# Banded attention: the third and fourth head's scores ahead of three projections, the last group's scores around the norm's transposes, adds ahead of lookups

## Chip, cores and metric

The kernel runs on one core of a Trainium2 chip. The metric is the device time of one execution in microseconds (us), as the median of three runs. The engines are called as the profile calls them: PE is TensorE (matrix products), DVE is VectorE, ACT is ScalarE, POOL is GpSimd, SP is the engine that only issues transfers here.

## The reference, cut to what matters

The program is a two-layer decoder; only the first of its six stages is touched: windowed attention with rotary positions, added to the residual stream. Per batch element (4 of them) there are 512 tokens of width 512, 16 query heads of width 128 in 4 groups, and one key/value head for each group.

```python
x = x + _L0_attn_ref(_layernorm(x, axis=-1), wq, wk, wv, wo)
...
q = jnp.einsum('bth,oh->bto', x, wq).reshape(B, T, Q_HEADS, HEAD_DIM)   # 16 heads
k = jnp.einsum('bth,oh->bto', x, wk).reshape(B, T, KV_HEADS, HEAD_DIM)  # 4 heads
v = jnp.einsum('bth,oh->bto', x, wv).reshape(B, T, KV_HEADS, HEAD_DIM)
q = _apply_rope(q, cos, sin)
k = _apply_rope(k, cos, sin)
scores = jnp.einsum('btgrd,bsgd->bgrts', qg, k) * scale
allowed = (idx[None, :] <= idx[:, None]) & (idx[:, None] - idx[None, :] <= WINDOW)   # WINDOW = 128
scores = jnp.where(allowed[None, None, None], scores, jnp.finfo(scores.dtype).min)
probs = jax.nn.softmax(scores, axis=-1)
out = jnp.einsum('bgrts,bsgd->btgrd', probs, v)
return jnp.einsum('bto,ho->bth', out, wo)
```

A later stage needs feed-forward weights that are given as 4-bit indices into a table of 16 values (`lut[gate_idx]` and so on). The kernel looks these up on DVE during the attention stage and stores them to memory for the later stage.

## The kernel before, in words

The attention stage is `stage_window_attention`. It makes one pass per batch element (three in a hardware loop, `more` true, and the last one outside of it, `more` false), and each pass goes over the 4 groups `g`. Each engine has its own program (`one_pass`, once for each engine); the engines meet through semaphores. No scheduler moves anything: the order on an engine is the order in which the code is written, and every engine runs its instructions strictly in that order.

The work of one group:

- Scores. PE computes the masked scores of the group's 4 heads (`scores`, lines 508 and 511) into two slots of PSUM. Heads 1 and 3 use one slot, heads 2 and 4 the other, so PE may begin head 3 only when ACT has taken the exponentials of head 1 out of the slot, and head 4 after those of head 2. DVE takes the row maxima (`maxima`, line 680), turns them into a bias (line 682), ACT takes the exponentials and row sums (`exponentials`, line 602), DVE the reciprocal of the sums (`inverse`, line 687), and POOL multiplies the probabilities by it (`probabilities`, line 759, four instructions for a head).
- Projections for the next group. Between the scores PE projects the next group's key k and its four queries q1 to q4 (`project`, line 491, `nxt` in the code). Each result goes through rotary encoding on three engines: ACT copies it with its halves exchanged (`swap`, lines 615 and 616), DVE multiplies the projection by the cosine (`rope`, line 675), POOL multiplies the exchanged copy by the sine (line 750) and adds both (line 753).
- Weighing. When the probabilities of all 4 heads are ready (PE waits for `prob_ready`), PE transposes them (`turn_probs`, line 521), multiplies by v (`weigh`, line 531), and by the output weights (line 574). DVE adds the four 128-row tiles to the residual x (line 729): these are "the adds".
- Four lookups on DVE in each group (`lookup.pick`, lines 364, 367 and 373, and `lookup.choose`, line 383). `pick` makes 4 masks and 8 choices between table values, `choose` reduces 8 candidates to 1 with 7 predicated copies; SP then stores the result and fetches new indices. A lookup is done by `pick` and `choose` of the same number, and one lookup must end before the next begins. Both inputs of a predicated copy, the mask and the values, are in SBUF.

In the third group of a pass DVE normalizes x for the next pass (`norm_stats`, `norm_apply`, with a power on POOL between them), and in the last group PE transposes it (`norm_tensor`, line 268) before the key and the queries of the next pass can be projected from it; ACT and DVE each copy two of the four transposed blocks (`features`). After the last group PE computes v for the next pass (`values`, line 541).

All PE results but the scores go through four PSUM banks in turn (`Ring`, by a list of steps). A step may write its bank only when the engine that read the step before it on that bank has released it. The four norm transposes follow the four output tiles on the ring, so the transposes of block k wait for add k.

The stage ends with a barrier of all engines, SP among them, and SP gets there only when the last lookup's store has landed (`sync_end`). The next stage issues its loads after that barrier.

## Time and profile before

| what | value |
|---|---|
| median of three runs | 2406.33 us (2403.66 to 2410.31) |
| the profiled execution's own time | 2406.55 us |
| its span, first to last instruction | 2404.8 us |
| attention stage from the first scores to the last add | 60.95 to 927.58 us of the span |
| PE, DVE, ACT, POOL busy over the whole span | 89%, 71%, 39%, 44% |
| mean granted clock of PE | 0.962 |

The profile is of one execution. Start times are us from the span's start. A row of the timeline gives start, length, engine, line, operation, what it writes and reads, how many such instructions in a row are merged into it, and in brackets how long the engine was idle just before and whose result ended that. A matmul in 32-bit is recorded as two parts, so four matmuls of 512 columns read "x8". PE's two clock levels are 2.4 GHz (1.0 in the column PEclk) and 1.2 GHz (0.5).

### The profile page before, as it was taken

Reading aid. Unit: us, or ns where it says so; the run is one execution under the profiler, and the core shown is the slowest. Engines: PE = TensorE matmul, PEld = TensorE weight load, DVE = VectorE, ACT = ScalarE, POOL = GpSimd, SP = SyncE. Lnnn points to the kernel's source line nnn. Section 1 sums busy time; section 2 is a strip of 40 time slices with the busy share of each in tenths; the row PEclk is TensorE's granted clock in tenths of the full one; section 3 lists DMA queues with packets and bytes.
Section 4 is the critical chain, followed back from the end, with each engine's and each line's share of the span. In section 5 each row is a group of like instructions: output and inputs, shape, how many; then the busy total and the mean of one; then the engine's idle time right before and its main releaser. Section 6 shows DMA issues by size and latency. Waiting matters only on the chain. (4 is left out here: it accounts for less than half of the span.)

```text
span 2404.8 us, 24923 instructions
## 1 busy us (share of the span) xinstructions
PE 2151.0 (89%) x7344; PEld 1108.7 (46%) x7344; DVE 1712.6 (71%) x2983; ACT 944.7 (39%) x1808; POOL 1048.7 (44%) x798
## 2 busy tenths in 40 slices
PE   6998999899999977997889898999789999999858
PEld 2554445454455543443555555465333433334234
DVE  1787788768876885786889889889546364654554
ACT  1443344333333433764655646465123232332311
POOL 2343354333333440322899998999511011010142
PEclk9999999999999998998999999999889999999979
DMA  7000000000000002455644526353332122221121
GB/s 263 19 19 18 19 20 20 18 18 22 22 18 19 23 23 90 159 186 214 266 162 166 197 105 210 127 203 108 107 80 78 41 77 57 70 70 46 52 109 53
DMA packets 95563, 214.87 MB, mean 89 GB/s; under 512 B 15832, under 2 KB 33112, under 8 KB 93032
## 3 DMA queue, kind: packets, MB, share of 16 engines
q1 hardware_dynamic: 77192, 156.18, 19.8%
q10 hardware_dynamic: 17760, 57.42, 6.7%
q8 instruction: 40, 0.66, 0.1%
q14 instruction: 59, 0.48, 0.1%
q0 software_dynamic: 512, 0.13, 0.0%
HBM read 146.30 MB, written 42.07 MB: 78 GB/s over the span
## 5 line engine op out<-in xcount | busy, mean ns | idle before, releaser
L759 POOL TENSOR_SCALAR a_prob<-a_prob,a_rsum 128x256 f32<-128x256 f32 x256 | 146.6, 590 | 467.3 <-DVE a_rsum L687 467.1
L1455 POOL TENSOR_TENSOR s_state<-s_b_rows,s_delta_u 128x1024 f32<-128x1024 f32 x128 | 303.5, 2384 | 36.9 <-DMA s_b_rows<-scan_bc 34.4
L1499 DVE TENSOR_TENSOR_SCAN s_state<-s_decay,s_state 128x512 f32<-128x512 f32 x256 | 304.9, 1211 | 15.5 <-ACT s_decay L1441 13.2
L1614 PE MATMUL c_bank<-c_xn_parts,c_w_parts 128*128 128x512 f32 (+1 forms) x1056 | 269.5, 405 | 6.2 <-DMA c_w_parts<-ffn_weights_lo 6.2
L1441 ACT ACTIVATE s_decay<-s_delta,s_a 128x512 f32<-128x512 f32 x256 | 173.5, 689 | 226.1 <-DVE s_state L1499 220.6
L491 PE MATMUL a_bank<-a_xn_t,a_wq 128*128 128x512 f32 x512 | 227.3, 592 | 0.0
L602 ACT ACTIVATE a_prob<-a_score,a_neg_m 128x256 f32<-128x256 f32 x256 | 117.6, 475 | 279.0 <-DVE a_neg_m L682 278.8
L1614 PEld LDWEIGHTS c_bank<-c_xn_parts,c_w_parts 128*128 128x128 f32 (+1 forms) x1056 | 196.3, 187 | 65.8 <-issue 20.3
L574 PE MATMUL a_bank<-a_wo,a_out_t 128*128 128x512 f32 x512 | 222.3, 593 | 0.0
L2049 ACT ACTIVATE d_prob_t<-d_score 128x512 f32<-128x512 f32 x256 | 138.9, 595 | 192.2 <-PE d_score L1931 191.1
L373 DVE TENSOR_SCALAR f_picks<-f_mask,f_lut_xor,f_lut 128x260 int32<-128x260 int32 x512 | 202.3, 468 | 9.6 <-DVE f_mask L367 0.5
L383 DVE COPY_PREDICATED f_picks<-f_mask,f_picks 128x260 int32<-128x260 int32 x448 | 177.7, 456 | 25.6
L2120 DVE TENSOR_REDUCE d_mx<-d_bank 128x1 f32<-128x512 f32 x256 | 158.6, 683 | 33.8 <-PE d_bank L1912 32.2
L2199 POOL DMA_DIRECT2D d_qs<-d_neg_t x16 | 8.8, 550 | 384.3 <-DVE d_neg_t L2128 384.3
L1627 PE MATMUL c_bank<-c_w_down,c_h_t 128*128 128x512 f32 (+1 forms) x352 | 163.3, 608 | 0.4
L1468 POOL TENSOR_TENSOR s_group<-s_group,s_state 128x1024 f32<-128x1024 f32 x64 | 152.7, 2385 | 6.3 <-DVE s_state L1507 6.3
L574 PEld LDWEIGHTS a_bank<-a_wo,a_out_t 128*128 128x128 f32 x512 | 97.4, 190 | 122.3 <-issue 122.3
L1507 DVE TENSOR_TENSOR s_state<-s_state,s_c 128x1024 f32<-128x1024 f32 x128 | 152.9, 1195 | 0.0
L491 PEld LDWEIGHTS a_bank<-a_xn_t,a_wq 128*128 128x128 f32 x512 | 97.4, 190 | 109.5 <-issue 108.0
L511 PE MATMUL a_score<-a_k_t,a_q_t 128*128 128x256 f32 (+1 forms) x512 | 132.5, 363 | 0.0
L1894 PE MATMUL d_bank<-d_xn_t,d_w 128*128 128x512 f32 x256 | 118.8, 609 | 4.4 <-DMA d_w<-in_d_w 2.2
L750 POOL TENSOR_TENSOR a_rope_b<-a_rope_b,a_sin 128x512 f32<-128x512 f32 x80 | 103.2, 1290 | 37.3 <-ACT a_rope_b L616 36.4
(210 smaller groups left out, 3646.2 us busy)
## 6 DMA issues: line engine op xcount, KB each, us to landing
s_b_rows<-scan_bc SPq DMA_DIRECT2D x64, 512.0 KB, 3.7
c_w_parts<-ffn_weights_hi ACTq DMA_DIRECT2D x39, 512.0 KB, 3.6
c_w_parts<-ffn_weights_lo ACTq DMA_DIRECT2D x39, 512.0 KB, 4.5
f_idx<-in_idx SPq DMA_DIRECT2D x64, 130.0 KB, 2.1
ffn_weights<-f_picks SPq DMA_DIRECT2D x64, 130.0 KB, 1.8
d_qs<-d_hi SPq DMA_DIRECT2D x128, 64.0 KB, 2.0
d_ks<-d_hi SPq DMA_DIRECT2D x128, 64.0 KB, 2.0
d_factor<-in_factors SPq DMA_DIRECT2D x16, 512.0 KB, 3.6
```

Source lines behind the costliest of these rows:

```text
L373: last = dve.tensor_scalar(picks[:, j, :], mask[:, 0, :], self.lut_xor[:, j:j + 1], self.lut[:, 2 * j:2 * j + 1], ALU.bitwise_and, ALU.bit ...
L383: last = self.nc.vector.copy_predicated(self.picks[:, j, :], self.mask[:, level + 1, :], self.picks[:, j + half, :])
L491: mm = nc.tensor.matmul(banks[b][:], w[:, k, :], xn_t[:, k, :], start=(k == 0), stop=(k == KD - 1))
L574: mm = nc.tensor.matmul(banks[b][:], out_t[:, tt, r * P:(r + 1) * P], wo[:, g * REPS + r, :], start=(r == 0), stop=(r == REPS - 1))
L1441: self.nc.scalar.activation(self.decay[u % 2][:], self.delta[:, h % 2, e, :], ACT.Exp, scale=self.a[:, h % 2 * 2 + e, n:n + 1]).then_inc(s ...
L1455: pool.tensor_tensor(self.state[:, s], row.broadcast_to([P, 2, T]), self.delta_u[:, h % 2], ALU.mult) \
L1468: pool.tensor_tensor(group, old if n == 1 else group, self.state[:, c % self.SLOTS], ALU.add) \
L1499: dve.tensor_tensor_scan(self.state[:, s, e, :], self.decay[u % 2][:], self.state[:, s, e, :], 0.0, ALU.mult, ALU.add).then_inc(self.scann ...
L1507: dve.tensor_tensor(self.state[:, s], self.state[:, s], row.broadcast_to([P, 2, T]), ALU.mult) \
L1614: mm = nc.tensor.matmul(banks[b][0:width[o], :], w_parts[:, n % SLOTS, w, at:at + width[o]], xn_parts[:, x_, k, :], start=((k, w, x_) == t ...
L1627: mm = nc.tensor.matmul(banks[b][:], h_t[0:width[o], o, tt * P:(tt + 1) * P], w_down[0:width[o], o, :], start=(o == 0), stop=(o == OT - 1))
L2120: nc.vector.tensor_reduce(mx[:, g, m // TT, m % TT:m % TT + 1], banks[b][:], AX_X, ALU.max) \
```

## The change

In the first three groups of a pass, and in the last group of the last pass, PE, ACT and POOL take the third and the fourth head directly after each other, and the projection of q2 comes behind them. (The code's `nxt[0:2]` are k and q1, `nxt[2:3]` is q2, `nxt[3:]` are q3 and q4.) DVE's maxima of head 4 and reciprocal of head 3 move ahead of the cosine product of q2.

In the last group of the first three passes the norm's transposes move from ahead of the first two heads' scores to behind them, and the last two heads' scores follow directly, all ahead of the projections. DVE and ACT copy the transposed blocks behind the exponentials of the first two heads, and DVE's first lookup moves behind the maxima of head 4.

In every group DVE's adds move: before, each of the first two adds stood behind a complete lookup (2, then 3), and the last two followed; now add 0 stands between `pick` and `choose` of lookup 2, add 1 behind that `choose`, adds 2 and 3 between `pick` and `choose` of lookup 3, and that `choose` is last. In the third group `pick` of lookup 1 now stands between the norm's statistics and its application.

```diff
@@ -420,14 +420,16 @@
     xn_steps = [("xn", k) for k in range(KD)]
     v_steps = [("v", tt) for tt in range(TT)]
 
+    def nxt_proj(g, more):
+        return proj((g + 1) % KV) if g + 1 < KV or more else []
+
     def steps(more):
 
         order = []
         for g in range(KV):
-            if g + 1 < KV:
-                order += proj(g + 1)
-            elif more:
-                order += xn_steps + proj(0)
+            if g == KV - 1 and more:
+                order += xn_steps
+            order += nxt_proj(g, more)
             order += [("turn", g, 0, 0), ("turn", g, 1, 0), ("turn", g, 1, 1), ("pv", g, 0),
                       ("turn", g, 2, 0), ("turn", g, 2, 1), ("pv", g, 1),
                       ("turn", g, 3, 0), ("turn", g, 3, 1), ("pv", g, 2), ("pv", g, 3)]
@@ -544,19 +546,18 @@
 
             def one_pass(i, more):
                 for g in range(KV):
-                    if g == KV - 1 and more:
-                        norm_tensor(nc, pe, norm, consts.ident, ring, banks, i + 1, in_pass=i)
-
                     ng = (g + 1) % KV
-                    nxt = proj(ng) if more or ng else []
+                    nxt = nxt_proj(g, more)
                     scores(i, g, (0, 1))
                     if ng == 0 and more:
+                        norm_tensor(nc, pe, norm, consts.ident, ring, banks, i + 1, in_pass=i)
+                        scores(i, g, (2, 3))
                         ring.wait_free(pe, i, consumed=xn_steps)
-                    project(ring, i, ng, nxt[0:2])
-                    scores(i, g, (2,))
-                    project(ring, i, ng, nxt[2:3])
-                    scores(i, g, (3,))
-                    project(ring, i, ng, nxt[3:])
+                        project(ring, i, ng, nxt[0:2])
+                    else:
+                        project(ring, i, ng, nxt[0:2])
+                        scores(i, g, (2, 3))
+                    project(ring, i, ng, nxt[2:])
                     pe.wait_ge(prob_ready, i * HEADS + (g + 1) * REPS)
                     turn_probs(i, g, 0, 0)
                     turn_probs(i, g, 1, 0)
@@ -625,17 +626,18 @@
 
             def one_pass(i, more):
                 for g in range(KV):
-                    if g == KV - 1 and more:
-                        features(ring, i)
                     ng = (g + 1) % KV
-                    nxt = proj(ng) if more or ng else []
+                    nxt = nxt_proj(g, more)
                     at = (ring, i, i + 1 if ng == 0 else i, ng)
                     exponentials(i, g, (0, 1))
-                    swap(*at, nxt[0:2])
-                    exponentials(i, g, (2,))
-                    swap(*at, nxt[2:3])
-                    exponentials(i, g, (3,))
-                    swap(*at, nxt[3:])
+                    if ng == 0 and more:
+                        features(ring, i)
+                        exponentials(i, g, (2, 3))
+                        swap(*at, nxt[0:2])
+                    else:
+                        swap(*at, nxt[0:2])
+                        exponentials(i, g, (2, 3))
+                    swap(*at, nxt[2:])
                     take(("turn", g, 0, 0), i, prob_t[:, 0, 0, :])
                     take(("turn", g, 1, 0), i, prob_t[:, 1, 0, :])
                     take(("turn", g, 1, 1), i, prob_t[:, 1, 1, :])
@@ -694,40 +696,57 @@
                 for tt in (0, 2):
                     take(("v", tt), i, v[:, tt, :], ring)
 
+            def add(i, g, tt):
+                b, turn = ring.at(("wo", g, tt), i)
+                dve.wait_ge(ring.full[b], turn)
+                nc.vector.tensor_tensor(x[:, i, tt, :], banks[b][:], x[:, i, tt, :], ALU.add) \
+                    .then_inc(ring.free[b], 1)
+
             def one_pass(i, more):
                 for g in range(KV):
-                    if g == KV - 1 and more:
-                        features(ring, i)
                     ng = (g + 1) % KV
-                    nxt = proj(ng) if more or ng else []
+                    nxt = nxt_proj(g, more)
                     at = (ring, i, i + 1 if ng == 0 else i, ng)
                     h = g * REPS
                     maxima(i, h)
                     maxima(i, h + 1)
-                    inverse(i, h)
-                    lookup.pick(i, g * TT)
-                    rope(*at, nxt[0:2])
-                    maxima(i, h + 2)
-                    inverse(i, h + 1)
+                    if ng == 0 and more:
+                        inverse(i, h)
+                        features(ring, i)
+                        maxima(i, h + 2)
+                        inverse(i, h + 1)
+                        maxima(i, h + 3)
+                        lookup.pick(i, g * TT)
+                        inverse(i, h + 2)
+                        rope(*at, nxt[0:2])
+                    else:
+                        inverse(i, h)
+                        lookup.pick(i, g * TT)
+                        rope(*at, nxt[0:2])
+                        maxima(i, h + 2)
+                        inverse(i, h + 1)
+                        maxima(i, h + 3)
+                        inverse(i, h + 2)
                     rope(*at, nxt[2:3])
-                    maxima(i, h + 3)
-                    inverse(i, h + 2)
                     lookup.choose(i, g * TT)
                     inverse(i, h + 3)
                     rope(*at, nxt[3:])
                     if g == KV - 2 and more:
                         wait_apart(dve, x_in, 16 * (B - 1), waited)
-                        norm_vector(nc, dve, norm, x, i + 1)
-                    lookup.pick(i, g * TT + 1)
+                        norm_stats(nc, dve, norm, x, i + 1)
+                        lookup.pick(i, g * TT + 1)
+                        norm_apply(nc, dve, norm, x, i + 1)
+                    else:
+                        lookup.pick(i, g * TT + 1)
                     lookup.choose(i, g * TT + 1)
-                    for tt in range(TT):
-                        if tt < 2:
-                            lookup.pick(i, g * TT + 2 + tt)
-                            lookup.choose(i, g * TT + 2 + tt)
-                        b, turn = ring.at(("wo", g, tt), i)
-                        dve.wait_ge(ring.full[b], turn)
-                        nc.vector.tensor_tensor(x[:, i, tt, :], banks[b][:], x[:, i, tt, :], ALU.add) \
-                            .then_inc(ring.free[b], 1)
+                    lookup.pick(i, g * TT + 2)
+                    add(i, g, 0)
+                    lookup.choose(i, g * TT + 2)
+                    add(i, g, 1)
+                    lookup.pick(i, g * TT + 3)
+                    add(i, g, 2)
+                    add(i, g, 3)
+                    lookup.choose(i, g * TT + 3)
                 if more:
                     values(ring, i)
 
@@ -763,14 +782,19 @@
             def one_pass(i, more):
                 for g in range(KV):
                     ng = (g + 1) % KV
-                    nxt = proj(ng) if more or ng else []
+                    nxt = nxt_proj(g, more)
                     at = (ring, i, i + 1 if ng == 0 else i, ng)
                     h = g * REPS
                     probabilities(i, h)
-                    rope_sums(*at, nxt[0:2])
-                    probabilities(i, h + 1)
+                    if ng == 0 and more:
+                        probabilities(i, h + 1)
+                        probabilities(i, h + 2)
+                        rope_sums(*at, nxt[0:2])
+                    else:
+                        rope_sums(*at, nxt[0:2])
+                        probabilities(i, h + 1)
+                        probabilities(i, h + 2)
                     rope_sums(*at, nxt[2:3])
-                    probabilities(i, h + 2)
                     probabilities(i, h + 3)
                     rope_sums(*at, nxt[3:])
                     if g == KV - 2 and more:
```

Three places show how the instructions now stand.

ACT, an ordinary group (a_score and a_prob are the scores and probabilities, a_bank a PSUM bank, a_rope_b the exchanged copy). Before, exponentials of head 3, exchange of q2 (two copies), exponentials of head 4:

```order
L600 REGISTER_ALU
L602 ACTIVATE a_prob,a_sums<-a_score,a_neg_m 128x256 x4
L615 COPY a_rope_b<-a_bank 64x512
L616 COPY a_rope_b<-a_bank 64x512
L600 REGISTER_ALU
L602 ACTIVATE a_prob,a_sums<-a_score,a_neg_m 128x256 x4
```

Now:

```order
L601 REGISTER_ALU
L603 ACTIVATE a_prob,a_sums<-a_score,a_neg_m 128x256 x4
L601 REGISTER_ALU
L603 ACTIVATE a_prob,a_sums<-a_score,a_neg_m 128x256 x4
L616 COPY a_rope_b<-a_bank 64x512
L617 COPY a_rope_b<-a_bank 64x512
```

The exchange of q2 moved behind the exponentials of head 4. DVE, the same place of the same group, from the reciprocal of head 2 to the first predicated copies. Before:

```order
L687 RECIPROCAL a_rsum<-a_sums 128x4
L675 TENSOR_TENSOR a_q_t<-a_bank,a_cos 128x512
L680 TENSOR_REDUCE a_mx<-a_score 128x4
L681 REGISTER_ALU
L682 TENSOR_SCALAR a_neg_m<-a_mx 128x4
L686 REGISTER_ALU
L687 RECIPROCAL a_rsum<-a_sums 128x4
L199 REGISTER_ALU
L383 COPY_PREDICATED f_picks<-f_mask,f_picks 128x260 x4
```

Now:

```order
L689 RECIPROCAL a_rsum<-a_sums 128x4
L682 TENSOR_REDUCE a_mx<-a_score 128x4
L683 REGISTER_ALU
L684 TENSOR_SCALAR a_neg_m<-a_mx 128x4
L688 REGISTER_ALU
L689 RECIPROCAL a_rsum<-a_sums 128x4
L677 TENSOR_TENSOR a_q_t<-a_bank,a_cos 128x512
L199 REGISTER_ALU
L383 COPY_PREDICATED f_picks<-f_mask,f_picks 128x260 x4
```

The cosine product of q2 (a_q_t) moved directly ahead of the predicated copies; behind the copies stands, before and now, the reciprocal of head 4.

DVE, the end of a group (here the second), from the last choices of lookup 3 to the next group's first maxima (x_res is the residual). Before:

```order
L372 ISA
L373 TENSOR_SCALAR f_picks<-f_mask,f_lut_xor,f_lut 128x260
L199 REGISTER_ALU
L383 COPY_PREDICATED f_picks<-f_mask,f_picks 128x260 x4
L199 REGISTER_ALU
L383 COPY_PREDICATED f_picks<-f_mask,f_picks 128x260 x2
L199 REGISTER_ALU
L383 COPY_PREDICATED f_picks<-f_mask,f_picks 128x260
L729 TENSOR_TENSOR x_res<-a_bank,x_res 128x512 x3
L680 TENSOR_REDUCE a_mx<-a_score 128x4
```

Now:

```order
L372 ISA
L373 TENSOR_SCALAR f_picks<-f_mask,f_lut_xor,f_lut 128x260
L702 TENSOR_TENSOR x_res<-a_bank,x_res 128x512 x2
L199 REGISTER_ALU
L383 COPY_PREDICATED f_picks<-f_mask,f_picks 128x260 x4
L199 REGISTER_ALU
L383 COPY_PREDICATED f_picks<-f_mask,f_picks 128x260 x2
L199 REGISTER_ALU
L383 COPY_PREDICATED f_picks<-f_mask,f_picks 128x260
L682 TENSOR_REDUCE a_mx<-a_score 128x4
```

The adds moved ahead of the seven predicated copies, and the maxima still follow both.

PE, the last group of a pass, behind the output products (L574, now L575). Before:

```order
L574 MATMUL a_bank<-a_wo,a_out_t 128x512 x16
L263 ISA
L266 REGISTER_ALU
L268 MATMUL a_bank<-ident,a_xn 128x128 x16
L501 REGISTER_ALU
L505 REGISTER_ALU
L508 MATMUL a_score<-mask_bf,ident_bf 128x256
```

Now the output products are followed by sixteen score instructions, and then come these (the first row is the last one of head 2, the last row the first one of head 3):

```order
L513 MATMUL a_score<-a_k_t,a_q_t 128x256
L263 ISA
L266 REGISTER_ALU
L268 MATMUL a_bank<-ident,a_xn 128x128 x16
L503 REGISTER_ALU
L507 REGISTER_ALU
L510 MATMUL a_score<-mask_bf,ident_bf 128x256
```

The sixteen transposes moved from ahead of the first head to ahead of the third.

## Rows read from the trace of the kernel before

**Rows 1.** Stretch, length, busy us (count) of PE, PEld, DVE, ACT, POOL, then PEclk.
```profile
60.95:927.58 866.63, 814.77 (x2696) 431.37 (x2696) 686.00 (x1598) 311.00 (x850) 340.65 (x409) 0.98 0.07 20
888.50:891.90 3.40, 3.39 (x12) 2.51 (x13) 3.25 (x11) 1.69 (x8) 2.28 (x4) 0.51 0.00 0
```

**Rows 2.** Waits of PE between 57 and 905 us: total, times, longest.
```profile
PE a_bank L521 <- POOL a_prob L759: 20.6, 15, 2.8
PE a_bank L268 <- DVE x_res L729: 19.5, 3, 6.5
```

**Rows 3.** Timeline of PE, third group of the first pass.
```profile
174.94 3.60 PE L491 MATMUL a_bank<-a_xn_t,a_wq 128*128 128x512 f32 x8
178.37 0.27 PE L508 MATMUL a_score<-mask_bf,ident_bf 128*128 128x256 bf16 x1
...
180.33 7.03 PE L491 MATMUL a_bank<-a_xn_t,a_wq 128*128 128x512 f32 x16
187.83 1.53 PE L521 MATMUL a_bank<-ident,a_prob 128*128 128x128 f32 x12 [0.47 <-POOL a_prob L759]
```

**Rows 4.** Timeline of ACT, same group: second copy of q2's exchange.
```profile
179.18 0.58 ACT L616 COPY a_rope_b<-a_bank 64x512 f32<-64x512 f32 x1
```

**Rows 5.** Timeline of DVE, same group.
```profile
179.78 0.69 DVE L675 TENSOR_TENSOR a_q_t<-a_bank,a_cos 128x512 f32<-128x512 f32 x1 [3.12 <-ACT a_rope_b L616]
...
182.47 3.17 DVE L383 COPY_PREDICATED f_picks<-f_mask,f_picks 128x260 int32<-128x260 int32 x7
```

**Rows 6.** Timeline of POOL, same group.
```profile
177.89 1.83 POOL L759 TENSOR_SCALAR a_prob<-a_prob,a_rsum 128x256 f32<-128x256 f32 x4
179.84 1.27 POOL L750 TENSOR_TENSOR a_rope_b<-a_rope_b,a_sin 128x512 f32<-128x512 f32 x1
181.18 1.26 POOL L753 TENSOR_TENSOR a_q_t<-a_q_t,a_rope_b 128x512 f32<-128x512 f32 x1
182.75 5.03 POOL L759 TENSOR_SCALAR a_prob<-a_prob,a_rsum 128x256 f32<-128x256 f32 x8 [0.31 <-DVE a_rsum L687]
```

**Rows 7.** Timeline of DVE, lookups 1 and 2 of the first group.
```profile
89.23 2.84 DVE L367 TENSOR_SCALAR f_mask<-f_idx 128x260 int32<-128x260 int32 x3
92.22 2.69 DVE L373 TENSOR_SCALAR f_picks<-f_mask,f_lut_xor,f_lut 128x260 int32<-128x260 int32 x8
95.06 3.01 DVE L383 COPY_PREDICATED f_picks<-f_mask,f_picks 128x260 int32<-128x260 int32 x7
...
98.43 0.70 DVE L367 TENSOR_SCALAR f_mask<-f_idx 128x260 int32<-128x260 int32 x3
```

**Rows 8.** Timeline of POOL, first group: its last instruction there.
```profile
90.60 1.32 POOL L753 TENSOR_TENSOR a_q_t<-a_q_t,a_rope_b 128x512 f32<-128x512 f32 x1 [0.16 <-POOL a_rope_b L750]
```

**Rows 9.** Timeline of PE, last group of the first pass.
```profile
218.04 2.82 PE L268 MATMUL a_bank<-ident,a_xn 128*128 128x128 f32 x12 [6.50 <-DVE x_res L729]
...
247.78 1.53 PE L521 MATMUL a_bank<-ident,a_prob 128*128 128x128 f32 x12 [0.81 <-POOL a_prob L759]
```

**Rows 10.** Timeline of DVE, end of the third group of the first pass.
```profile
189.21 2.46 DVE L213 BATCH_NORM_STATS2 a_stats<-x_res 128x6 f32 x4
...
194.21 1.92 DVE L228 TENSOR_SCALAR a_xn<-x_res,a_mean_var,a_rstd 128x512 f32 x4 [1.14 <-POOL a_rstd L257]
...
217.31 1.88 DVE L729 TENSOR_TENSOR x_res<-a_bank,x_res 128x512 f32 x3
```

**Rows 11.** Costliest groups in the stage: count, busy us, mean ns.
```profile
L602 ACT ACTIVATE a_prob<-a_score,a_neg_m 128x256 f32<-128x256 f32 x256 | 117.6, 475 | 279.0 <-DVE a_neg_m L682 278.8
```

**Rows 12.** Timeline of PE, last group of the last pass: first row of head 3.
```profile
888.51 0.35 PE L508 MATMUL a_score<-mask_bf,ident_bf 128*128 128x256 bf16 x1 [3.17 <-ACT a_prob L602]
```

**Rows 13.** End of the stage: DVE's last add, SP's next load.
```profile
926.89 0.69 DVE L729 TENSOR_TENSOR x_res<-a_bank,x_res 128x512 f32<-128x512 f32 x1 [1.63 <-PE a_bank L574]
928.59 0.41 SPq L937 DMA_DIRECT2D b_ctx_t<-in_ctx_t  x1
```

**Rows 14.** Transfers by line: KB each, median us from issue to landing.
```profile
ffn_weights<-f_picks SPq DMA_DIRECT2D x64, 130.0 KB, 1.8
```

## The prediction

> **What bounds the kernel now.** I read the busy time by stretches first. In the attention stage PE is busy 814.77 of 866.63 us [rows 1], so PE sets the pace, and only its idle time and its slow clock can be won: about 52 us and what the clock costs. DVE is busy 686.00 us and is the nearest rival.
>
> The list of PE's waits says where the idle time lies [rows 2]. Fifteen times it waits for POOL's last probabilities before it transposes them, 20.6 us in all, at most 2.8 us each. Three times, once in each pass but the last, it waits for DVE's add before the norm's transposes, 19.5 us in all. Behind such a wait PE's clock is at its lower level: the twelve transposes after a wait of 6.50 us take 2.82 us, while twelve transposes behind a short wait take 1.53 us [rows 3, 9].
>
> Then I read one ordinary group engine by engine, to see what ends last before the probabilities. PE's q3 and q4 end near 187.4 us, and POOL ends a moment later: PE waits 0.47 us and goes on at 187.83 us [rows 3]. Followed back, POOL's last eight instructions run 182.75 to 187.78 us [rows 6]; the second four wait for the reciprocal of head 4, which DVE makes behind its seven predicated copies, 182.47 to 185.64 us [rows 5]; the copies stand behind the maxima of head 4, and these behind the cosine product of q2 at 179.78 us, for which DVE waited 3.12 us. That product waits for ACT's exchange, over at 179.76 us [rows 4]. So the chain is exchange of q2, DVE's copies, POOL's last head, PE. It ends within half a microsecond of PE's own work.
>
> **The change, part by part.**
>
> *Ordinary groups, 12 times on the path.* The instructions are the same; their order differs. Head 4's scores take 1.96 us (178.37, where q2's four matmuls end, to 180.33 us) [rows 3]. They now stand ahead of q2, so q2 is done 1.96 us later, and its exchange too, since ACT is just then done with head 4's exponentials: four of 475 ns, 1.9 us [rows 11], behind those of head 3, which were over when the exchange began near 178.6 us [rows 4]. The exchange ends at 181.7 us in place of 179.76. The cosine product ends at 182.4 us, and the copies begin there: as before (182.47), because the maxima that used to stand between the two are already done. What was won ahead of the chain is lost on the exchange.
>
> What is new is POOL's work beside the copies. Before, it was scaling heads 3 and 4, and now head 3 is done early and POOL runs q2's sine product (1.27 us, from 181.8 us) and sum (1.26 us, to 184.4 us) [rows 6]. Whether copies can run beside these is not shown: no predicated copy of this trace meets such a product. The bounds are:
>
> - They don't disturb each other. So it is for the cosine product, which reads PSUM and SBUF: 0.69 us beside POOL's product, and that takes 1.27 us [rows 5, 6]. Then the copies take 3.01 us [rows 7], the reciprocal is out at 185.6 us, POOL needs 0.3 us to begin and 1.83 us for the head [rows 6], and PE goes on at 187.6 us: 0.2 us won.
> - The copy waits for POOL's whole instruction. So it is for DVE's masks: three take 0.70 us alone and 2.84 us beside POOL, and end at 92.07 us, just after POOL's sum (91.92 us) [rows 7, 8]. Then the first copy is done at 183.2 us, with the end of the sine product; one more may slip in ahead of the sum; the next is done near 184.6 us; the four or five left take 0.43 us each (3.01/7). The copies end at 186.3 to 186.7 us and PE goes on at 188.4 to 188.9 us: 0.6 to 1.1 us lost.
>
> The nearest rows are the copies themselves beside POOL's scaling: seven take 3.17 in place of 3.01 us, and the eight scalings take 5.03 us where four alone take 1.83 [rows 5 to 7], so the first four took 3.2 us. Each holds up the other; I take the second bound, 0.9 us.
>
> On this point the Trainium skill, page "SBUF — State Buffer", section "Who interferes with whom", has a rule: a VectorE instruction with two SBUF inputs contends with a GpSimd instruction that reads SBUF, and the one that starts second is held until the first is over. By that rule the second bound holds, and the sum below; without it the sum is the first rival's, 2400.5 us. The masks agree with it (2.84 us beside POOL, 0.70 alone); no row here shows it for copies beside a two-input product.
>
> The 0.9 us don't add up twelve times. In the second group of a pass the wait is the longest (2.8 us) because DVE comes late out of the four lookups of the first; a PE that is itself 0.9 us later makes DVE less late. POOL's last two sums and products, which hold up the next masks, also move back, and cost DVE about 0.3 us. I count 0.9 for the first group, 0.3 for the second and 0.9 for the third: **2 us in each of four passes, 8 us lost**. Bounds: 2 us won (0.2 twelve times, nothing else) to 13 us lost (1.1 twelve times).
>
> *The last group of three passes.* Take the first pass, 0.9 us late. PE began the wait of 6.50 us at 218.04 - 6.50 = 211.5 us with four transposes done (0.5 us), so its output products ended near 211.0 us [rows 9], now 211.9. It makes the first two heads' scores (3.9 us) and the transposes (twelve take 1.53 us [rows 3], so sixteen about 2.0). The adds are done by then, so the old wait is gone. PE is ready at 217.8 us. Head 3 now needs the slot of head 1, so head 1's maxima and exponentials must be over, and DVE reaches the maxima only behind all four lookups and adds: from the norm's statistics at 189.21 us to the last add at 219.19 us it took 30.0 us [rows 10]. The same work takes 28.9 us when the wait of 1.14 us for POOL is covered by a lookup, and up to 30 us when POOL's later sums hold up its masks. I take 218.8 us. Maxima and bias (1.4 us) and four exponentials (1.9 us [rows 11]) end at 222.1 us: **PE waits 4.3 us in a new place**, and behind it on PE stand two heads' scores and five projections, for which ACT's exchanges and POOL's sums wait in turn. A wait of 3.17 us for the same reason stands in the last pass [rows 12], and behind it the clock is 0.51 for 3.4 us [rows 1], which costs 1.7 us. So heads 3 and 4 take 3.9 + 1.7 us, and all scores are done at 227.7 us. Five projections of 3.43 us end at 244.9 us.
>
> The probabilities are later than that. Behind the scores come maxima and bias of head 4 (1.5 us), the lookup's masks and choices (about 1.0 + 2.7 with gaps 3.8 us [rows 7]) and only then the reciprocal of head 3: 233.4 us. POOL scales head 3 (1.8 us) and makes three products and three sums (six of 1.3 us): 243.4 us. DVE's copies run beside the last three of them, from about 240 us, and end near 244.7 us if held up; then the reciprocal, 0.3 us and 1.83 us give 247.0 us, plus PE's own start. Before, PE went on at 247.78 us [rows 9], which with the 0.9 us of lateness is 248.7. **Won: about 1.4 us, three times, 4 us.** Bounds: 0 (a second stretch at half clock, or slower copies) to 3.2 us (copies not held up; then POOL's sums set the end, 243.4 + 2.1 us).
>
> *The end of the stage.* In the last group DVE waits for PE, not the other way: the last add waits 1.63 us, ends at 927.58 us, and SP's first load of the next stage is issued at 928.59 us [rows 13]. The last lookup's copies and store were over by then. Now the copies stand behind that add: 3.0 us [rows 7], then the store, 1.8 us to land and some 0.1 us to issue [rows 14]. SP reaches the barrier 4.9 us later, and nothing covers it, since the next stage's loads stand behind the barrier. **5 us lost**; 4 to 5.5 are the bounds.
>
> *At nothing:* the adds ahead of lookups 2 and 3 in ordinary groups, since the next projections find their banks free in both orders (the waits of PE list no such wait [rows 2]); v's products likewise.
>
> *Sum:* 8 - 4 + 5 = 9 us on the profiled execution's 2406.55 us, which lies 0.2 us from the median of 2406.33. **2415.5 us.**
>
> **Rivals.**
>
> 1. *Copies aren't held up by POOL's products.* For it: the cosine product isn't [rows 5, 6]. Against it: copies and scalings lengthen each other [rows 5 to 7]. It decides when a copy beside a product takes under 0.5 us. Ordinary groups win 2 us, the last groups 9 us (three times 3), the end costs 5: 2400.5 us, 6 us faster.
> 2. *The norm's wait goes and nothing takes its place*, as when DVE reaches the maxima with PE's first head. Then 6.5 us and some 2 us of slow clock are won in three passes, 25 us; with 8 and 5 lost, 2394 us: **faster**. Against it: 30 us of DVE's work between the same two points [rows 10]. It would need 4 us less.
> 3. *The longer waits cost the clock too.* In the second groups waits of 2.8 us grow past 3 us, near the 3.17 us behind which the clock fell [rows 12]: 1.7 us in each of four passes, and the full 13 us in ordinary groups: 2425 us.
>
> **How the numbers follow.** A measurement of this kernel tells about 0.3%, 7 us, from no change: 2399.1 to 2413.5 us is "same". My case has 0.60, with its own range of 2409 to 2421 us; the first rival 0.19, the second 0.06, the third 0.15. Faster: half of the first rival, whose middle lies at the limit, and the second, 0.15. Slower: most of my case and the third, 0.57. Same: 0.28. The range reaches past the middles of the first and the third rival and leaves out the second and their far tails, under 0.2: 2398 to 2427 us.
>
> **What would show it.** Right: q2's exchange 2 us later against q1, predicated copies of lookup 0 at 4 us or more beside POOL's products, PE's fifteen waits for probabilities grown to 30 us or more, no wait for the norm's transposes but three of about 4 us for exponentials of head 1, and SP's first load of the next stage some 6 us behind the last add. Wrong: copies of 3.0 us beside the products, or a PE that finds head 1's exponentials done.

## The result, and the profile after

The changed kernel takes **2449.0 us** (median of four runs, 2443.2 to 2450.3) beside 2407.5 us for the kernel before, run with it: a ratio of 1.0169, 95% interval 1.0147 to 1.0191. It is slower, as forecast, but by 42 us and not by 9, and it lies beyond the end of the range (2427 us).

PE's waits in the attention stage and at the head of the next, in the changed kernel (total us, times, longest):

```profile
PE a_bank L523 <- POOL a_prob L778: 44.7, 15, 3.9
PE m_bank L1015 <- DMA m_w_in<-in_m_in_t: 12.0, 1, 12.0
PE a_score L510 <- ACT a_prob L603: 9.5, 4, 3.1
```

The fifteen waits for probabilities have doubled [rows 2]: 44.7 in place of 20.6 us. The norm's waits of 6.5 us are gone; three waits of 2.0 to 2.2 us for head 1's exponentials stand in their place (the fourth, 3.1 us, was there [rows 12]).

Where the 42 us lie is read from the stage cut into pieces. Of the kernel before, the three ordinary groups of each pass, the last groups of the first three passes, and the stretch from the next stage's first matmul to the end of the feed-forward stage (length, PE busy and count, granted clock):

```profile
60.95:210.66 149.71, 145.96 (x486) 0.99 0.07 19
210.66:284.08 73.42, 66.11 (x211) 0.95 0.08 22
284.08:434.09 150.01, 144.77 (x488) 1.00 0.06 18
434.09:506.74 72.65, 65.36 (x211) 0.95 0.08 22
506.74:656.97 150.23, 146.49 (x488) 0.99 0.06 18
656.97:730.80 73.83, 66.49 (x210) 0.93 0.08 22
730.80:880.83 150.03, 144.64 (x488) 1.00 0.07 20
...
926.02:934.10 8.08, 0.85 (x3) 0.72 0.53 165
934.10:1729.10 795.00, 696.55 (x2192) 0.95 0.46 167
```

The same pieces of the changed kernel:

```profile
60.39:217.88 157.49, 148.57 (x486) 0.97 0.07 20
217.88:288.27 70.39, 65.43 (x211) 0.98 0.07 20
288.27:446.74 158.47, 149.56 (x488) 0.96 0.07 19
446.74:520.19 73.45, 68.33 (x212) 0.93 0.06 18
520.19:678.80 158.61, 149.71 (x488) 0.96 0.07 19
678.80:750.58 71.78, 66.69 (x212) 0.95 0.07 19
750.58:909.46 158.88, 149.70 (x488) 0.96 0.07 19
...
954.67:967.50 12.83, 0.87 (x3) 0.64 0.36 113
967.50:1771.50 804.00, 706.55 (x2192) 0.94 0.47 165
```

The ordinary groups take 633.45 in place of 599.98 us, **33.5 us more**. PE is busy in them for 597.5 in place of 581.9 us, so 15.7 us are the same matmuls at a lower granted clock (0.96 or 0.97 for 0.99 or 1.00), and 17.8 us are idle time. The three last groups take 215.6 in place of 219.9 us, 4.3 us won. From the last matmul of the stage to the first of the next it is 12.83 in place of 8.08 us, 4.8 us lost. The stretch behind is 9.0 us longer, and PE's idle time in it is about the same (98.5 us before, 97.5 now): its matmuls were slower. The other stretches together are 0.6 us shorter.

One ordinary group shows the first cause: PE, DVE and POOL in the third group of the first pass, as in [rows 3, 5, 6].

```profile
193.98 2.82 PE L523 MATMUL a_bank<-ident,a_prob 128*128 128x128 f32 x12 [3.05 <-POOL a_prob L778]
```
```profile
183.54 0.18 DVE L689 RECIPROCAL a_rsum<-a_sums 128x4 f32<-128x4 f32 x1 [0.61 <-ACT a_prob L603]
186.56 0.69 DVE L677 TENSOR_TENSOR a_q_t<-a_bank,a_cos 128x512 f32<-128x512 f32 x1 [2.84 <-ACT a_rope_b L617]
187.17 4.64 DVE L383 COPY_PREDICATED f_picks<-f_mask,f_picks 128x260 int32<-128x260 int32 x7
191.71 0.17 DVE L689 RECIPROCAL a_rsum<-a_sums 128x4 f32<-128x4 f32 x1
```
```profile
182.84 3.67 POOL L778 TENSOR_SCALAR a_prob<-a_prob,a_rsum 128x256 f32<-128x256 f32 x8
186.61 1.27 POOL L769 TENSOR_TENSOR a_rope_b<-a_rope_b,a_sin 128x512 f32<-128x512 f32 x1
187.96 1.33 POOL L772 TENSOR_TENSOR a_q_t<-a_q_t,a_rope_b 128x512 f32<-128x512 f32 x1
192.08 1.84 POOL L778 TENSOR_SCALAR a_prob<-a_prob,a_rsum 128x256 f32<-128x256 f32 x4 [2.79 <-DVE a_rsum L689]
```

The seven copies lie beside POOL's product and sum for q2 and take 4.64 us; before they took 3.17 beside the scaling. Three of them one by one (the first, the second, the third):

```profile
187.17 1.02 DVE L383 COPY_PREDICATED f_picks<-f_mask,f_picks 128x260 int32<-128x260 int32 x1
188.09 1.51 DVE L383 COPY_PREDICATED f_picks<-f_mask,f_picks 128x260 int32<-128x260 int32 x1
189.50 0.44 DVE L383 COPY_PREDICATED f_picks<-f_mask,f_picks 128x260 int32<-128x260 int32 x1
```

The first copy ends at 188.19 us, 0.3 us behind the end of POOL's product (187.88), the second at 189.60, 0.3 us behind the end of its sum (189.29); the other five take 0.44 or 0.45 us each. POOL then stands idle for 2.79 us until the reciprocal behind the copies, and PE, ready at 190.93, waits 3.05 us. Ahead of all that DVE is idle for 2.84 us, with POOL on instructions of one tensor each. And PE's twelve transposes take 2.82 us, where before they took 1.53.

### The profile page after: what moved, and what is told of

The parts are those of the page before. It is cut to its first block and busy times, and to the rows that moved or that the text cites. A ratio compares the mean times of both kernels' runs of the same rounds, so it can differ in the third digit from the quotient of the medians.

```text
span 2447.1 us, 24908 instructions
## 1 busy us (share of the span) xinstructions
PE 2178.2 (89%) x7344; PEld 1128.7 (46%) x7344; DVE 1735.3 (71%) x2983; ACT 946.9 (39%) x1808; POOL 1031.9 (42%) x798
## 5 line engine op out<-in xcount | busy, mean ns | idle before, releaser
L778 POOL TENSOR_SCALAR a_prob<-a_prob,a_rsum 128x256 f32<-128x256 f32 x256 | 128.1, 523 | 518.6 <-DVE a_rsum L689 518.6
L1638 PE MATMUL c_bank<-c_xn_parts,c_w_parts 128*128 128x512 f32 (+1 forms) x1056 | 274.8, 411 | 6.9 <-DMA c_w_parts<-ffn_weights_lo 6.8
L373 DVE TENSOR_SCALAR f_picks<-f_mask,f_lut_xor,f_lut 128x260 int32<-128x260 int32 x512 | 220.0, 502 | 9.6 <-DVE f_mask L367 1.4
L575 PE MATMUL a_bank<-a_wo,a_out_t 128*128 128x512 f32 x512 | 222.3, 592 | 0.0
L383 DVE COPY_PREDICATED f_picks<-f_mask,f_picks 128x260 int32<-128x260 int32 x448 | 200.9, 508 | 21.6 <-DVE f_picks L383 1.5
L575 PEld LDWEIGHTS a_bank<-a_wo,a_out_t 128*128 128x128 f32 x512 | 97.3, 190 | 122.5 <-issue 122.5
L523 PE MATMUL a_bank<-ident,a_prob 128*128 128x128 f32 x448 | 78.0, 337 | 52.6 <-POOL a_prob L778 44.7
```

Of the source, the lines that this page charges most:

```text
L373: last = dve.tensor_scalar(picks[:, j, :], mask[:, 0, :], self.lut_xor[:, j:j + 1], self.lut[:, 2 * j:2 * j + 1], ALU.bitwise_and, ALU.bit ...
L383: last = self.nc.vector.copy_predicated(self.picks[:, j, :], self.mask[:, level + 1, :], self.picks[:, j + half, :])
L575: mm = nc.tensor.matmul(banks[b][:], out_t[:, tt, r * P:(r + 1) * P], wo[:, g * REPS + r, :], start=(r == 0), stop=(r == REPS - 1))
L1638: mm = nc.tensor.matmul(banks[b][0:width[o], :], w_parts[:, n % SLOTS, w, at:at + width[o]], xn_parts[:, x_, k, :], start=((k, w, x_) == t ...
```

## The experiments

**Theory.** The copies beside q2's product and sum are 1.47 us longer, each wait grows by that or more, and the clock that falls behind longer waits costs as much again. **Rivals.** The adds moved ahead of the lookups cause the waits: their last copies run into the next group's maxima. Or: the copies are long wherever they lie. Or: PE's slower matmuls have nothing to do with its waits.

**1. The first edit alone.** On the kernel before, in all groups but the last of three passes:

```diff
-                    scores(i, g, (2,))
-                    project(ring, i, ng, nxt[2:3])
-                    scores(i, g, (3,))
-                    project(ring, i, ng, nxt[3:])
+                    scores(i, g, (2, 3))
+                    project(ring, i, ng, nxt[2:])
```
(and ACT's, DVE's and POOL's orders of the change.)

> The kernel before with the first edit alone (scores of heads 3 and 4 together in every group but the last of the first three passes, with the orders of ScalarE, VectorE and GpSimd that go with it). Theory: q2's two products on GpSimd now lie beside the seven copies of the group's first lookup, these take 4.6 us in place of 3.2, the fourth head's probabilities come later by that much, and each wait of TensorE that has grown past some 2 us is followed by a stretch at half clock. Then the twelve waits on probabilities are at 1.9 (first group) and 2 to 4 (second and third), their sum over the stage goes from 20.6 to 36 or more, the norm's three waits stay at 6.5, and the time is 2407.5 + 33 = 2440 us (2432 to 2448). Rival (the extra waits come from the adds, whose last copies run into the next group's maxima): no more than the 1 us or so of a changed phase, 2405 to 2412 us.

Measured: 2431.8 us, ratio 1.0090 (1.0071 to 1.0109), 21 us slower. PE's waits:

```profile
PE a_bank L521 <- POOL a_prob L778: 34.3, 15, 4.0
PE a_bank L268 <- DVE x_res L748: 14.7, 3, 4.9
```

The ordinary groups wait 1.95, 4.0 and 1.95 us, as the theory has it; the copies take 4.64 us in all twelve. The norm's waits were forecast unchanged and fell to 4.9 us, as PE comes later to the same adds. The time is 8 us below the forecast: that edit alone is about half of the 42 us. In its trace the twelve ordinary groups take 625.3 us, 25.3 more than before, and the three last groups are 4.4 us shorter. The first groups of passes 2 to 4 ran at a clock of 1.00 here behind the same wait of 1.95 us, behind which the changed kernel's ran at 0.97 in passes 2 and 3.

**2. All but the first edit.** The changed kernel, ordinary groups in the old order:

```diff
                         project(ring, i, ng, nxt[0:2])
-                        scores(i, g, (2, 3))
-                    project(ring, i, ng, nxt[2:])
+                        scores(i, g, (2,))
+                        project(ring, i, ng, nxt[2:3])
+                        scores(i, g, (3,))
+                    project(ring, i, ng, nxt[2:] if ng == 0 and more else nxt[3:])
```

> The changed kernel with the first edit taken back: the ordinary groups have their scores, exponentials, maxima, inverses and probabilities in the order of before, and the last groups, the adds and the norm are as changed. Theory: the ordinary groups' waits go back to the order of 0.5, 2.8 and 2, the copies of the first lookup to 3.2 us, and the time falls by the 33 us that the ordinary groups lost, to 2416 us (2405 to 2424). Rival (the adds cause the waits): 2440 to 2449 us, with the second and third groups still waiting 3 to 4 us.

Measured: 2415.3 us, ratio 1.0028 (1.0012 to 1.0043). The theory's figure: taking back the first edit takes back 34 of the 42 us. Alone it costs 21, so some 12 us come only when it stands together with the rest. In this run's trace the ordinary groups take 600.6 us, as before (600.0), so all of the 33.5 us there need the first edit: it adds 25.3 us to them alone and 33.5 together with the adds.

**3. The adds alone.** The kernel before with the adds of the change:

```diff
-                    for tt in range(TT):
-                        if tt < 2:
-                            lookup.pick(i, g * TT + 2 + tt)
-                            lookup.choose(i, g * TT + 2 + tt)
-                        ...
+                    lookup.pick(i, g * TT + 2)
+                    add(i, g, 0)
+                    lookup.choose(i, g * TT + 2)
+                    add(i, g, 1)
+                    lookup.pick(i, g * TT + 3)
+                    add(i, g, 2)
+                    add(i, g, 3)
+                    lookup.choose(i, g * TT + 3)
```

> The kernel before with the adds moved ahead of the lookups alone, the norm and the scores untouched. Theory: the norm's transposes wait on banks that the adds free, so the three waits of 6.5 us shrink to about 1 us, 3 x 5.5 = 16 us won with a part of the half-clock stretches behind them; the first exponentials of each group come up to 1.4 us later, some 0.5 us lost in eight groups, 4 us; the end of the stage loses 5 us as the last store waits for the copies behind the last add: 2407.5 - 16 + 4 + 5 = 2400 us (2392 to 2412). Rival (the adds cause the longer waits of the ordinary groups): the second and third groups wait 3 to 4 us, and the time is 2425 us or more.

Measured: 2410.7 us, ratio 1.0002 (0.9988 to 1.0016), no change, near the upper end of what was expected.

```profile
PE a_bank L521 <- POOL a_prob L765: 21.8, 15, 2.5
PE a_bank L268 <- DVE x_res L700: 9.8, 3, 3.3
```

The norm's waits are halved (forecast 1 us, got 3.3), and the 5 us at the stage's end are paid: PE waits 12.1 us for the next stage's weights. The ordinary groups take 600.3 us beside 600.0, so the adds by themselves don't make them longer, and that rival falls as the main cause. But they change what a late PE costs. Before, the third group's wait is 0.47, 1.97, 0.47 and 2.23 us in the four passes: it is short where PE's clock had fallen behind the second group's wait (granted clock 0.97 in passes 1 and 3, 1.00 in 2 and 4), and the second and third groups together take 101.2 to 101.5 us in every pass. The slower PE was absorbed. With the adds alone the third wait is 1.83 to 1.86 us in passes 1 to 3 (2.18 in the fourth), and the two groups together take 102.2 and 102.0 us behind the fallen clock and 100.7 us in passes 2 and 4. A late PE is passed on; that this is because DVE's last two lookups now stand behind adds that wait for PE is argued from the order of the code. The change pays it on top of the longer copies: its third groups wait 3.0 us in passes 1 to 3 and 3.7 in the fourth.

**4. What holds the copies up.** The changed kernel with its order, but q2's product and sum on POOL read one tensor and a column:

```diff
-                    nc.gpsimd.tensor_tensor(rope_b[:, s, :], rope_b[:, s, :], sin2[:], ALU.mult)
+                    nc.gpsimd.tensor_scalar(rope_b[:, s, :], rope_b[:, s, :], sin2[:, 0:1], 1.0, ALU.mult, ALU.mult)
```
(The sum likewise, for q2 in the ordinary groups alone; cut to the two operations, POOL's waits ahead of them stand in instructions of their own. q2 isn't rotated then.)

> The changed kernel, but in the ordinary groups GpSimd's product and sum for q2 take one tensor and a column in place of two tensors, so q2 isn't rotated as the reference has it (wrong values; the order of all instructions is as in the changed kernel). Theory (two tensors read by GpSimd hold up the copies beside them): the seven copies of the first lookup go from 4.64 to 3.2 to 3.5 us, the first group's wait falls from 1.95 to 0.5 us and the second's and third's by 1.2 to 1.5 each, about 17 us of waits in twelve groups, with the half-clock stretches of the first groups on top: 2449 - 17 - 6 = 2426 us (2418 to 2434). Rival (the copies are late because VectorE reaches them 1 us later than before, behind q2's product, and would take as long beside anything): copies stay at 4.4 us or more, and the time at 2444 to 2450 us.

Measured: 2412.3 us, 37 us below the changed kernel. DVE in the third group:

```profile
185.38 0.69 DVE L677 TENSOR_TENSOR a_q_t<-a_bank,a_cos 128x512 f32<-128x512 f32 x1 [2.84 <-ACT a_rope_b L617]
185.99 3.52 DVE L383 COPY_PREDICATED f_picks<-f_mask,f_picks 128x260 int32<-128x260 int32 x7
```

POOL beside them:

```profile
185.55 0.70 POOL L770 TENSOR_SCALAR a_rope_b<-a_rope_b,a_sin 128x512 f32<-128x512 f32 x1 [0.22 <-ACT a_rope_b L617]
186.54 1.13 POOL L774 TENSOR_SCALAR a_q_t<-a_q_t,a_cos 128x512 f32<-128x512 f32 x1 [0.30 <-POOL a_rope_b L770]
```

The copies stand in the same place, behind the same wait of 2.84 us, and take 3.52 us; the rival's 4.4 is excluded. POOL's two instructions hold them up, then. Whether it is their second tensor or their length (1.27 and 1.33 us, here 0.70 and 1.13) this run doesn't separate. The ordinary waits are 0.83, 2.4 and 1.93 us (0.83, 2.0 and 2.0 in the last pass), and the ordinary groups take 605.7 us: 27.8 of the 33.5 us are gone. 37 us is more than I expected (23): behind the shorter waits the clock came back, in the first groups of passes 2 to 4 (1.00) and in the last groups of passes 2 and 3, which I had not counted (68.7 us each in place of 73.5 and 71.8). Without q2's two-tensor work the kernel is as fast as the kernel before (ratio 1.0007, 0.9993 to 1.0020).

**5. Only the place of the copies.** The changed kernel, one line moved on DVE:

```diff
-                    rope(*at, nxt[2:3])
                     lookup.choose(i, g * TT)
+                    rope(*at, nxt[2:3])
                     inverse(i, h + 3)
```

> The changed kernel with one line of VectorE moved: the copies of a group's first lookup stand ahead of q2's rotation, where VectorE sits idle for 2.8 to 3.1 us until ScalarE has swapped q2, and GpSimd works on probabilities with one tensor each. Theory: the copies take 3.2 us there in place of 4.64, the fourth head's inverse comes 3 to 4 us earlier, GpSimd does its probabilities behind q2's sum, and the ordinary groups' waits fall from 1.95, 3.9, 3.0 to 0, 0.7, 0.3 or so; with the half clock behind them that is 31 + 15 us of the stage: 2449 - 46 = 2403 us (2396 to 2414). Rival (the copies are long wherever they lie, and the waits come from the order of the exponentials): 2440 us or more.

Measured: 2405.1 us, ratio 0.9977 (0.9966 to 0.9987). One line gives back 44 us. DVE and POOL in the third group:

```profile
182.29 3.46 DVE L383 COPY_PREDICATED f_picks<-f_mask,f_picks 128x260 int32<-128x260 int32 x7
185.64 0.68 DVE L677 TENSOR_TENSOR a_q_t<-a_bank,a_cos 128x512 f32<-128x512 f32 x1
186.24 0.17 DVE L689 RECIPROCAL a_rsum<-a_sums 128x4 f32<-128x4 f32 x1
```
```profile
181.38 5.15 POOL L778 TENSOR_SCALAR a_prob<-a_prob,a_rsum 128x256 f32<-128x256 f32 x8
186.50 1.27 POOL L769 TENSOR_TENSOR a_rope_b<-a_rope_b,a_sin 128x512 f32<-128x512 f32 x1
187.85 1.27 POOL L772 TENSOR_TENSOR a_q_t<-a_q_t,a_rope_b 128x512 f32<-128x512 f32 x1
189.09 1.85 POOL L778 TENSOR_SCALAR a_prob<-a_prob,a_rsum 128x256 f32<-128x256 f32 x4
```

The copies fill the time in which DVE had been idle, and end 0.7 us behind q2's exchange (185.75 and 185.08 us). They hold up the scaling beside them (5.15 us for eight in place of 3.67), and POOL then works without a gap until head 4 is scaled at 190.94 us, for which PE waits. It is the same in the second group. So the second and third waits are longer than the 0.7 and 0.3 us I expected: 2.0 and 1.5 us. The first group's is 0.4 us, for a bank that DVE's product holds. The ordinary groups take 595.5 us, 4.5 less than before.

**6. The clock by itself.** The changed kernel with idle work for PE ahead of each wait on probabilities:

```diff
+                    pe.wait_ge(exp_done[0], i * PER_SLOT + (g * REPS + 2) // 2 + 2)
+                    for _ in range((14, 28, 22, 20)[g] if more or ng else 0):
+                        nc.tensor.transpose(score[0][:, 0, 0:P], consts.ident[:], consts.ident[:])
                     pe.wait_ge(prob_ready, i * HEADS + (g + 1) * REPS)
```
(The first line waits until ACT has taken the exponentials of head 3 out of the bank that the transposes write.)

> The changed kernel with work for TensorE in its waits: ahead of each wait on the group's probabilities (not in the very last group) 14, 28, 22 and 20 transposes of the identity go to a score bank that is free by then, and nobody reads them. They take 1.8, 3.6, 2.8 and 2.6 us at full clock, about as long as the waits. Theory (half of the ordinary groups' loss is the clock that falls behind a wait): the turns behind the waits take 1.53 us and the groups' granted clock goes from 0.94 to 0.97 to 1.00, 15 us in the ordinary groups and some 3 in the last ones, and the time is 2449 - 17 = 2432 us (2425 to 2438) though nothing else has become faster. Rival (TensorE's longer instructions have another cause than its idle time): 2447 to 2455 us.

Measured: 2428.5 us, 20.5 us below the changed kernel, with PE doing more. The ordinary groups of the four passes:

```profile
61.18:214.18 153.00, 151.08 (x549) 1.00 0.07 20
285.68:439.07 153.39, 151.50 (x552) 1.00 0.07 19
510.76:664.16 153.40, 151.51 (x552) 1.00 0.07 19
735.94:889.60 153.66, 151.50 (x551) 1.00 0.07 20
```

They add up to 613.45 us in place of 633.45, all at full clock. So PE's slower matmuls come from its waits, and that rival falls: filling the waits gives back 20 of the 33.5 us that the ordinary groups lost.

**7. The fourth head earlier still.** The version of 5 in ordinary groups, and head 4's reciprocal and scaling ahead of q2's rotation:

```diff
                         probabilities(i, h + 2)
-                    rope_sums(*at, nxt[2:3])
-                    probabilities(i, h + 3)
+                        probabilities(i, h + 3)
+                    rope_sums(*at, nxt[2:3])
```
(POOL's part in ordinary groups; DVE's reciprocal likewise. In the last groups of three passes both follow head 3's at once.)

> The changed kernel with the fourth head brought forward: in ordinary groups VectorE does the copies of the first lookup and then the fourth head's inverse ahead of q2's rotation, and GpSimd the fourth head's probabilities ahead of q2's products; in the last groups the fourth inverse follows the third at once, and its probabilities stand ahead of k's products. Theory: the waits on probabilities vanish in all 15 groups (44.7 us to under 3), the half clock behind them too (15 to 18 us), and the waits for head 1's exponentials and the stage's end (9.5 and 5 us) stay: 2449 - 42 - 16 = 2391 us (2382 to 2400). Rival (q2's later sum becomes a new wait, for the next group's scores or for a bank): TensorE waits 1 us or more per group at its scores or projections, and the time is 2410 us or more.

Measured: 2420.8 us, ratio 1.0045 (1.0027 to 1.0063); the rival had it. PE's waits, and ACT in the second group:

```profile
PE a_bank L533 <- DVE a_q_t L677: 21.7, 12, 2.6
PE a_bank L523 <- DVE a_q_t L677: 10.7, 3, 3.6
```
```profile
137.74 0.58 ACT L616 COPY a_rope_b<-a_bank 64x512 f32<-64x512 f32 x1 [4.16 <-POOL a_q_t L776]
```

No wait for probabilities is left, and 32 us of waits for a bank have come. ACT may exchange q4 only when POOL has added q2 out of the same buffer; with head 4 scaled first, q2's sum is late, ACT waits 4.16 us for it, DVE's product of q4 is late, and that product holds the bank. So POOL's scaling and its sums compete for the same moment.

**8. With the last copies ahead of the last add**, on top of 7 (`choose` of the fourth lookup between the adds 2 and 3).

> As the kernel before this in the list, and the copies of a group's fourth lookup stand ahead of the group's last add, as far as the order allows. Theory: the last store of the stage no longer waits for copies behind the last add, TensorE's wait for the next stage's weights goes from 12.0 to 7.2 us, the groups themselves don't change since the same copies then lie ahead of one add: 2391 - 5 = 2386 us (2377 to 2395). Rival (the last add, later by up to 3 us, keeps a bank, and TensorE waits for it at the norm's transposes or the projections): no gain or a loss against the kernel before this.

Measured: 2412.1 us, ratio 1.0007 (0.9998 to 1.0017), 8.6 us below the kernel of 7. The gain is a little more than the 5 us expected, from a start 30 us off. The wait for the next stage's weights is 9.5 us and not 7.2; the last copies still stand behind add 2.

**9. Copies deferred into the next group**, last groups regrouped:

```diff
                     maxima(i, h + 1)
+                    if g:
+                        lookup.choose(i, g * TT - 1)
```
(further edits as the expectation tells them.)

> The version with the copies of the first lookup ahead of q2's rotation in ordinary groups, and three more moves: the copies of a group's fourth lookup stand behind the first two maxima of the next group (in the last group of a pass ahead of its last add); in the last groups the inverses of heads 3 and 4 come at once and GpSimd scales all four heads ahead of k's products; there the first lookup's masks stand behind k's rotation and its copies behind the last rotation. Theory: the first maxima of the second to fourth groups come 3 us earlier, so the waits for head 1's exponentials (3.5 us in three groups) go, the probabilities of the last groups (2.4 us) are done long before TensorE wants them, the second and third groups' waits fall from 2.0 and 1.5 to about 1.2 and 0.8, and the stage's end wins 2.5 us or more: 2405 - 10.5 - 7 - 5 - 2.5, with some 5 us of clock: 2377 us (2368 to 2392). Rival (VectorE has no room: work moved out of the start of a group makes its end late, and TensorE waits for a bank at the turns or for the adds instead): waits on a bank that VectorE holds of 1 us or more in most groups, and 2395 to 2410 us.

Measured: 2403.9 us, ratio 0.9983 (0.9967 to 0.9999): one half right. The last groups take 65.8 us in place of 70 to 73. The second and third groups wait 3.1 and 2.8 us, more than in 5 (2.0 and 1.5): at the start of the second group DVE now idles for 1.16 and 0.53 us until PE's scores are there, where in 5 it ran the copies, and the copies have to be done later.

**10. The end of the stage alone.** The changed kernel, with the last lookup's copies ahead of the adds 2 and 3 in the very last group.

> The changed kernel, but in the very last group the copies of the last lookup stand ahead of the last two adds, so that the last store no longer waits behind the last add. Theory: TensorE's wait for the next stage's weights goes from 12.0 to 7.2 us or a little more, nothing else changes, 2449 - 4.8 = 2444 us (2441 to 2447). Rival (the next stage's start is set by something else): 12 us of wait, and 2447 to 2451 us. The stages behind this one took 9 us longer in the changed kernel's profile than in that of before; if that comes from the late store it goes too, and the time is 2435 us.

Measured: 2440.7 us, ratio 1.0129 (1.0112 to 1.0146).

```profile
PE m_bank L1019 <- DMA m_w_in<-in_m_in_t: 8.9, 1, 8.9
```

The wait fell from 12.0 to 8.9 us, so the store behind the last add is a cause of it, if not of the whole; in 11, with the old order there, it is 7.1 us. The stretch from the next stage's first matmul to the end of the feed-forward stage is still 803.65 us, so the 9 us there don't come from the late store. The time fell by 8 us, between the two expectations; 3.1 us of it are that wait, and no row places the rest (the profile, 2445.7 us, is of the slowest of the four runs).

**11. The good halves together:** ordinary groups as in 5, last groups of the first three passes as in 9 (but their own last copies behind the last add), and only the third group's last copies deferred; the very last group's adds and lookups as before.

> Ordinary groups as in the version with the copies ahead of q2's rotation, last groups of the first three passes as in the regrouped version (the third group's last copies behind the first two maxima, all four heads scaled ahead of k's products), and the very last group with its adds and lookups in the order of the kernel before. Theory: TensorE waits 0.4, 2.0 and 1.5 us in the ordinary groups and 0.7 and 1.4 in the last ones, 12 us less than with the copies ahead alone in three passes together, and 7.2 us for the next stage's weights: 2405 - 12 - 5 = 2388 us (2380 to 2400), faster than before by 0.9%. Rival (what is taken from the last groups' waits comes back in the first group of the next pass, since VectorE does the same work): the sum of waits stays, 2400 to 2408 us.

Measured: **2386.6 us**, ratio 0.9895 (0.9878 to 0.9912), 1% faster than the kernel before and 2.6% faster than the changed one.

```profile
PE a_bank L523 <- POOL a_prob L793: 14.0, 8, 2.1
...
PE m_bank L1031 <- DMA m_w_in<-in_m_in_t: 7.1, 1, 7.1
...
PE a_bank L533 <- DVE a_q_t L677: 6.0, 7, 1.4
PE a_score L510 <- ACT a_prob L603: 5.1, 4, 3.1
```

Of the changed kernel's 54 us of waits in the stage (44.7 + 9.5) 25 are left, waits for banks among them, in smaller pieces.

## Why the prediction was wrong

**The step that failed** is *Ordinary groups*: "2 us in each of four passes, 8 us lost". It is 33.5 us. The mechanism was right: the copies beside q2's product and sum are held up, and 4, 5 and the rows above show it. The rule quoted there from the Trainium skill (page "SBUF — State Buffer", section "Who interferes with whom") now has its row: 4.64 us, with each of the first two copies held until POOL's instruction was over. (The masks that the prediction calls in agreement read one tensor, f_idx, so they are no case of a rule for two inputs.) The size was off in three ways:

- *0.9 us for the first group* measured 1.47 to 1.49. POOL's sum ends 2.1 us after the copies' start (in the third group's lines; I had 2.0), but 2.5 us of copies are left then (187.96 + 1.33 to 191.81); I had taken 1.9 to 2.3. No copy slipped in between the product and the sum.
- *"The 0.9 us don't add up twelve times"*, with 0.3 for the second group and 0.9 for the third, measured 0.8 to 1.1 and 1.1 to 2.6. A later PE no longer made DVE less late. For the third group experiment 3 shows it of the adds, which I had put at nothing in ordinary groups. PE's idle time grew by 17.8 us where 8 were forecast.
- *No term for the clock.* The third rival had this mechanism, priced it at 1.7 us in the second groups alone and got 0.15. (Its terms, 13 + 6.8 - 4 + 5, add up to 2427 us and not to 2425, the very end of the range.) The first groups' waits grew from 0.47 to 1.95 us, the third groups' to 3.0 us and more, and the granted clock was below 1.00 in eleven of the twelve groups, where it had been so in two: 15.7 us more of PE's busy time, and 20 us in all that filling the waits gives back. My own rows had shown the price (1.53 and 2.82 us for the same transposes [rows 3, 9]); I used it for the last groups only.

The sum also has no term for the stages behind, where the profile shows 9.0 us more (see *Open*).

**Right:**

- *Last groups:* 4 us forecast, 4.3 measured, in part by luck: the forecast was 1.4 us in each, and the three passes won 3.0, lost 0.8 and won 2.1 us, with PE busy for 0.7 us less, 3.0 more and 0.2 more. The norm's wait went and a wait for head 1's exponentials came, 2.0 to 2.2 us where I had 4.3; the probabilities' wait rose from 0.8 to 2.9 us, and the copies there take 5.55 us where I had 4.7. The parts differ, the sum agrees.
- *End of the stage:* 5 us forecast, 4.8 measured; SP's first load is issued 5.8 us behind the last add, where I had some 6.
- *First rival* (copies not held up): wrong, 4.64 us. *Second* (the norm's wait goes and nothing comes): wrong, PE finds head 1 unfinished in all three groups.

**Open:** the 9 us in the stages behind. PE's idle time is the same there and its clock lower (0.94 for 0.95). Nothing in those stages was changed. In the profiles of the other kernels the same stretch takes from 797 (experiment 3, with the late store) to 808 us (experiment 9, which is faster than before), so neither the time of the attention stage nor the late store sets it. Followed matmul by matmul, the stretch falls behind that of before in steps of 1.7 us or less, many at the same places in the profiles of 9, 10 and 11. What brings them, no run here tells. The profile of before, 2406.55 us, is of one of its faster runs: 25 runs beside the first experiments have a median of 2410.4 us. So some 4 of the 9 us may be that one profile; the runs of one kernel spread by 2 to 15 us (experiments 6 and 7).

## What to carry to other kernels

When a reorder frees an engine early, look at what that engine does next and who shares SBUF with it at that moment: here a GpSimd that finished scaling early put its two-tensor products beside VectorE's copies, on whose end the whole group hung. Price a longer TensorE wait with the clock behind it, which here cost about as much again (15.7 us of slower matmuls beside 17.8 us of idle time). And before moving work out of a wait, see whether the waiting engine has other work to put into it: one line that put the copies into VectorE's idle 2.8 us was worth 44 us.

## What the runs showed that I had not expected

- The clock doesn't follow from a wait's length alone: behind a wait of 1.95 us the first groups of passes 2 and 3 ran at a granted clock of 0.97 in the changed kernel and at 1.00 with the first edit alone. In the kernel before, behind waits of 2.7 to 2.8 us, the second groups ran at 0.97 in passes 1 and 3 and at 1.00 in 2 and 4.
- TensorE can be made faster by giving it more to do: 64 useless transposes in each pass's ordinary groups shortened these from 158 to 153 us.
- Copies and one-tensor scaling share without a long stall (3.2 to 3.5 us for the seven copies, 3.01 alone), but both pay: eight scalings take 5.15 us beside them and 3.67 us alone.
